# Attention and mixture-of-experts layer on one core: in the first chunk, the copies of the second eight heads' keys and queries wait for the first unit's rows of maxima

## The chip, the cores and the metric

The kernel runs on one core of one Trainium2 chip. A core has a matrix engine (TensorE, PE in the rows), a vector engine (VectorE, DVE), a scalar engine (ScalarE, ACT), a general engine (GpSimd, POOL), and a sync engine (SyncE, SP) that here only issues DMAs; each runs its own list of instructions in order, and they meet at semaphores. The metric is the time of one execution on the device in microseconds; lower is better.

## The reference, cut to what matters

One layer on 2048 tokens of 256 numbers: causal attention with 16 heads of 16 numbers, keys and values from a latent of 64, rotary embedding on 12 of 16 numbers of each head; then a layer norm, then a mixture of 16 experts (the best two for each token) with a shared expert, and a layer norm again.

```python
q = (x @ Wq).reshape(B, S, HEADS, HEAD_DIM).transpose(0, 2, 1, 3)
c_kv = x @ Wkv_down
k = (c_kv @ Wk_up).reshape(B, S, HEADS, HEAD_DIM).transpose(0, 2, 1, 3)
v = (c_kv @ Wv_up).reshape(B, S, HEADS, HEAD_DIM).transpose(0, 2, 1, 3)
...
qf = jnp.concatenate([q_nope, q_rope], axis=-1)
kf = jnp.concatenate([k_nope, k_rope], axis=-1)
scores = jnp.einsum('bhqd,bhkd->bhqk', qf, kf) * scale
scores = jnp.where(causal, -jnp.inf, scores)
weights = jax.nn.softmax(scores, axis=-1)
out = jnp.einsum('bhqk,bhkd->bhqd', weights, v)
...
x = _layernorm(x + _L0_attn_ref(x, ...), axis=-1)
x = _layernorm(x + _L0_ffn_ref(x, ...), axis=-1)
```

## The kernel before, in words

Attention goes by chunks of 512 queries (four) and in each by units of four heads (four a chunk, 16 in all). A unit takes steps, one for each block of 128 keys up to its chunk's end: 4 steps for each unit of chunk 0, 8 for those of chunk 1. In a step, `score_head` (line 1092) multiplies one block of keys with the 512 queries of each head, ScalarE takes the exponential (line 857), GpSimd clears what lies above the diagonal (`mask`, line 709), and every second step TensorE multiplies the probabilities of two steps with the values (`values`, line 1112). Scores go round three banks, so TensorE can be three heads ahead of ScalarE.

The softmax needs the maximum of each query's row before its first score. So each unit is computed twice: first `max_bank` (lines 1055 and 1060) makes its scores, VectorE takes maxima (lines 1312 and 1318) and folds them (1329), TensorE turns the column into rows (1035), VectorE writes them negated in two parts to `m_rows` (1372, 1373), and ScalarE's queue copies these two rows into `q_stack` below the queries (`store_maxima`, line 807, semaphore `m_stacked`, 16 for each of the two DMAs). The score matmul has 98 rows then, against 96 before. TensorE waits for `m_stacked` before a unit's first score.

Keys and queries are made in pieces. Piece n of a chunk: 0 keys and 1 queries of heads 0 to 7, 2 keys and 3 queries of heads 8 to 15. A piece is two jobs `("rope", c, 2n)` and `("rope", c, 2n + 1)`: TensorE projects (lines 970, 975, 983), ScalarE copies the bank to `rope_raw`, which has two buffers (line 819), the rotation makes three products and sums (`rotate`, lines 502, 503, 507; on VectorE in chunk 0, on GpSimd after it), and GpSimd splits the result in two parts in `kq_stage` (lines 642, 643, semaphore `kq_ready`). SP then runs `store_piece`: six DMAs that write the piece's parts, three copies of each half, to DRAM (line 552), and after a piece of queries the load of `k_stack` (line 559). `load_q` (line 530) loads the queries of a unit into `q_stack`. `load_tables` (line 541) loads the cosine and sine tables of the next chunk, which `rotate` needs.

The order of SP in chunk 0: pieces 0 and 1, `k_stack`, `load_q` of units 0 and 1, pieces 2 and 3, `k_stack`, `load_q` of units 2 and 3, `load_tables(1)`, then pieces 0 and 1 of chunk 1, `k_stack`, the next chunk's x, `load_q(4)`. A planner at the head of the program sets which bank of maxima and which job goes to which step, the same for all engines. By it the jobs before the first step are all of chunk 0's projections, the first latent of chunk 1, the maxima of unit 0, and ("rope", 1, 0); steps 0, 1 and 2 have ("rope", 1, 1), (1, 2) and (1, 3), step 2 also the maxima of unit 1. Unit 2's banks start in step 3, and unit 4's, the first of chunk 1, in step 9. After GpSimd's part of ("rope", 1, 0) come the load of the first tokens (line 653) and the mask of step 0, and from there masks and pieces by turns.

Of the kernel before, what the change touches and what calls it, by code (L numbers as in the profile page):

```python
# [59 lines left out]
def build_program(nc, t, out):  # L60
# [90 lines left out]
    for u in range(4, UNITS):  # L151
        c, g = divmod(u, UNITS_PER_CHUNK)
# [65 lines left out]
    with ExitStack() as ctx:  # L218
# [6 lines left out]
        def sem(name):  # L225
            return ctx.enter_context(nc.semaphore(name))
# [124 lines left out]
        m_stacked = sem("m_stacked")  # L351
# [158 lines left out]
        def _(sp):  # L510
# [32 lines left out]
            def store_piece(c, n):  # L543

                piece = 4 * c + n
                m, is_q = n // 2, n % 2

                sp.wait_ge(kq_ready, 2 * (piece + 1))
                for two in range(2):
                    rows = slice(two * (P // 2), (two + 1) * (P // 2))  # L550
                    for copy, part in enumerate((0, 1, 0) if is_q else (0, 0, 1)):
                        sp.dma_start(kq_dram[c, n, two, copy], kq_stage[rows, piece % 2, part].bitcast(F32))\
                          .then_inc(kq_stored[is_q], 16)
                if is_q:

                    sp.wait_ge(kq_stored[0], 16 * 6 * (piece // 2 + 1))
                    if piece > 1:
                        sp.wait_ge(k_stacked, 16 * (piece // 2))
                    sp.dma_start(k_stack[0:STACK, 4 * m:4 * m + 4, c * CH:(c + 1) * CH].bitcast(F32),
                                 kq_dram[c, n - 1].rearrange("two copy (d j) n -> (two copy d) j n", j=GH)).then_inc(k_stacked, 16)  # L560
                    sp.wait_ge(kq_stored[1], 16 * 6 * (piece // 2 + 1))
# [22 lines left out]
            for s in range(-1, END):  # L584
                for job in aux_at.get(s, ()):
                    if job[0] == "rope" and job[2] % 2:
                        store_piece(job[1], job[2] // 2)
                        if job[1] == 0 and job[2] % 4 == 3:
                            load_q(job[2] // 4 * 2)
                            load_q(job[2] // 4 * 2 + 1)  # L590
                        if job[2] == 3 and 0 < job[1] < NCH - 1:
                            load_chunk(job[1] + 1)
                        if job[2] == 7 and job[1] + 1 < NCH:
                            load_tables(job[1] + 1)
                for u in range(4, UNITS):
                    if q_load_at[u] == s:
                        load_q(u)

                if s == FREE_AT:
                    load_small()  # L600
                if s == FREE_AT + 20:
                    load_rows()
# [1214 lines left out]
```

## Time and profile before

| | us |
|---|---|
| median of 3 timed runs | 838.95 (837.67 to 840.08) |
| the profiled execution's own time | 838.23 |
| its span | 836.5 |
| TensorE busy | 720.1 (86%) |
| VectorE busy | 577.2 (69%) |
| ScalarE busy | 396.4 (47%) |
| GpSimd busy | 243.6 (29%) |

The span is the time from the first to the last instruction in the profile of one execution. Busy time says how much work an engine had, not that it was waited for: that is read from the chain of waits and from the timelines. A time in brackets behind an instruction is the idle time of its engine just ahead of it, with what ended it; "issue" there means nothing that the profile names.

### The profile page before, as it was taken

The numbers are of one execution on the slowest core, as the hardware profiler recorded it, in microseconds if no ns is written. First come the engines' busy times: TensorE is split into PE (matmuls) and PEld (weight loads), VectorE is DVE, ScalarE is ACT, GpSimd is POOL, SyncE is SP. The second block draws the span as 40 slices with busy tenths as digits, with TensorE's granted clock in tenths as the row PEclk, the third lists the DMA queues.
The fourth block names the chain that finished last, engine by engine and source line by source line (L and its number), as shares of the span: only waits on it lengthen the run. The fifth ranks groups of instructions, "written<-read, shape, count | busy, mean of one in ns | idle before, by whom it ended". The sixth has DMA issues, their size and how long they took to land.

```text
span 836.5 us, 13801 instructions
## 1 busy us (share of the span) xinstructions
PE 720.1 (86%) x4150; PEld 473.3 (57%) x4151; DVE 577.2 (69%) x1402; ACT 396.4 (47%) x848; POOL 243.6 (29%) x321
## 2 busy tenths in 40 slices
PE   4579899999999999999799999999839599999920
PEld 3467675664755666466355565544728466666610
DVE  6745779878789877776688888636616566665645
ACT  3125465555665756576466666668213122222203
POOL 6317172431261043107011010101650323333323
PEclk9659899999999999999899999999979799999965
DMA  4764315250051105001514800002950223333244
GB/s 130 170 158 109 97 40 139 80 130 20 2 128 51 52 1 138 16 1 39 132 43 123 263 2 1 20 2 69 318 207 2 83 77 94 97 95 95 82 170 157
DMA packets 43783, 75.96 MB, mean 91 GB/s; under 512 B 6004, under 2 KB 23668, under 8 KB 42860
## 3 DMA queue, kind: packets, MB, share of 16 engines
q1 hardware_dynamic: 36396, 57.75, 25.3%
q0 software_dynamic: 4896, 13.67, 4.8%
q10 hardware_dynamic: 2432, 3.80, 1.3%
q8 instruction: 31, 0.51, 0.3%
q14 instruction: 28, 0.23, 0.1%
HBM read 41.91 MB, written 32.93 MB: 89 GB/s over the span
## 4 chain that ended last, share of the span: by engine, by line
PE 64%; DVE 12%; issue 9%; DMA 6%; POOL 3%; ACT 3%; SPq 1%; ACTq 1%; another core or an unknown queue 1%; POOLq 0%; DVEq 0%
PE banks_ps L1055 15%; PE banks_ps L1112 14%; PE banks_ps L1092 12%; PE banks_ps L1152 7%; PE banks_ps L1188 5%; DVE mx L1318 4%; PE banks_ps L970 2%; PE banks_ps L1060 2%; PE banks_ps L1247 1%; ACT probs L857 1%; PE banks_ps L1165 1%; DMA q_stack<-kq_split 1%; DVE base L1739 1%; PE banks_ps L1176 1%; DMA token_y<-ys,dest 1%
## 5 line engine op out<-in xcount | busy, mean ns | idle before, releaser
L857 ACT ACTIVATE probs<-banks_ps 128x512 f32<-128x512 f32 (+3 forms) x640 | 302.4, 546 | 189.8 <-PE banks_ps L1092 173.8
L1318 DVE TENSOR_REDUCE mx<-banks_ps 128x1 f32<-128x512 f32 (+3 forms) x576 | 307.8, 593 | 72.4 <-PE banks_ps L1055 71.6
L1055 PE MATMUL banks_ps<-k_stack,q_stack 96*128 96x512 f32 (+3 forms) x832 | 251.2, 366 | 11.2 <-issue 5.6
L1092 PE MATMUL banks_ps<-q_stack,k_stack 98*128 98x512 f32 (+3 forms) x640 | 242.3, 397 | 17.3 <-ACT probs L857 11.4
L1055 PEld LDWEIGHTS banks_ps<-k_stack,q_stack 96*128 96x128 f32 x832 | 151.8, 202 | 89.8 <-issue 34.5
L1092 PEld LDWEIGHTS banks_ps<-q_stack,k_stack 98*128 98x128 f32 x640 | 122.7, 195 | 54.4 <-ACT probs L857 31.5
L1112 PE MATMUL banks_ps<-probs,v_ones 128*17 128x512 f32 (+3 forms) x1280 | 136.6, 543 | 1.1 <-POOL probs L709 0.9
L709 POOL TENSOR_SCALAR_AFFINE_SELECT probs<-probs 128x512 f32<-128x512 f32 x64 | 40.9, 639 | 325.0 <-ACT probs L857 324.8
L767 POOL DMA_INDIRECT token_y<-ys,dest x47 | 45.6, 970 | 96.8 <-DVE ys L1716 53.1
L1152 PE MATMUL banks_ps<-w_up_sb,xg_t 128*128 x188 | 67.9, 484 | 0.3 <-DVE hidden L1650 0.3
L1112 PEld LDWEIGHTS banks_ps<-probs,v_ones 128*17 128x17 f32 x1280 | 29.5, 98 | 67.5 <-issue 36.8
L1312 DVE TENSOR_REDUCE mx<-banks_ps 128x4 f32<-128x512 f32 x64 | 44.2, 690 | 31.0 <-PE banks_ps L1060 29.7
L1188 PE MATMUL banks_ps<-w_dn_sb,hidden_t 88*128 x188 | 49.3, 386 | 0.5 <-DVE ys L1716 0.5
L1703 DVE SCALAR_TENSOR_TENSOR part_w<-xg,expert_f 128x1 f32<-128x1 f32 x94 | 16.4, 216 | 44.3 <-DMA token_y<-ys,dest 39.5
L910 ACT ACTIVATE xg_t<-banks_ps 128x256 f32<-128x256 f32 x47 | 18.0, 383 | 56.9 <-PE banks_ps L1247 47.8
L1152 PEld LDWEIGHTS banks_ps<-w_up_sb,xg_t 128*128 128x128 f32 x188 | 32.4, 192 | 15.1 <-issue 1.7
L819 ACT ACTIVATE rope_raw<-banks_ps 128x512 f32<-128x512 f32 x32 | 19.2, 599 | 42.3 <-issue 20.3
L878 ACT ACTIVATE silu<-banks_ps 128x176 f32<-128x176 f32 x47 | 14.9, 317 | 45.7 <-PE banks_ps L1152 44.7
L1201 PE MATMUL banks_ps<-shared_dn,hidden_split 128*128 128x256 f32 (+1 forms) x144 | 22.5, 311 | 14.4 <-DVE hidden_split L1673 9.4
L1188 PEld LDWEIGHTS banks_ps<-w_dn_sb,hidden_t 88*128 88x128 f32 x188 | 32.3, 192 | 3.7 <-issue 1.0
L1165 PE MATMUL banks_ps<-x1t_first,shared_up 128*128 128x512 f32 (+1 forms) x108 | 27.5, 399 | 3.9 <-issue 3.9
L1201 PEld LDWEIGHTS banks_ps<-shared_dn,hidden_split 128*128 128x128 f32 (+1 forms) x144 | 20.6, 212 | 17.6 <-issue 8.6
(182 smaller groups left out, 727.8 us busy)
## 6 DMA issues: line engine op xcount, KB each, us to landing
kq_split<-kq_stage SPq DMA_DIRECT2D x96, 128.0 KB, 2.4
k_stack<-kq_split SPq DMA_DIRECT2D x8, 768.0 KB, 6.2
q_stack<-kq_split SPq DMA_DIRECT2D x32, 192.0 KB, 4.9
xg<-slot_x SPq DMA_DIRECT2D x47, 130.0 KB
slot_x<-blank SPq DMA_DIRECT2D x11, 520.0 KB, 8.6
w_up_sb<-w_up SPq DMA_DIRECT2D x4, 1408.0 KB
w_dn_sb<-w_dn SPq DMA_DIRECT2D x4, 704.0 KB
x_raw<-xT SPq DMA_DIRECT2D x4, 512.0 KB, 6.3
```

The source lines that it names most:

```text
L709: nc.gpsimd.affine_select(out=v, in_=v, compare_op=ALU.is_ge, fill=0.0, base=0, pattern=[[0, GH], [1, P]], channel_multiplier=-1).then_inc ...
L767: pool.indirect_dma_start(out=token_y, out_offset=bass.IndirectOffsetOnAxis(ap=dest[:, r:r + 1], axis=0), in_=ys[:, r, :], in_offset=None) ...
L857: nc.scalar.activation(probs[:, s % PROB_BUFS, h, off:CH], score_bank(n)[:, off:CH], ACT.Exp)\
L1055: ins = nc.tensor.matmul(dst[:, at:at + keys], q_stack[0:STACK, u % 4, h, tile * P:(tile + 1) * P], k_stack[0:STACK, pair, kb * CH + k0:kb ...
L1092: nc.tensor.matmul(score_bank(n)[:, off:CH], k_stack[:, 2 * g + h // 2, b * P:(b + 1) * P], q_stack[:, u % 4, h, off:CH], start=True, stop ...
L1112: last = nc.tensor.matmul(pv_ps[32 * h:32 * h + DH + 1, off:CH], v_ones[:, b, GH * g + h, :], probs[:, s % PROB_BUFS, h, off:CH], start=(b ...
L1152: last = nc.tensor.matmul(gate_ps[par][:, 0:2 * INTER], x_of(k), w_up[:, e, k, :], start=(k == 0), stop=(k == KT - 1))
L1165: last = nc.tensor.matmul(bank[n % 2][0:rows], shared_up[:, w, k, half, at:at + rows], x_of[:, a, k, tok], start=(m == 0), stop=(m == 3 * ...
L1188: last = nc.tensor.matmul(y_ps[par][:, 0:E], hidden_t[:, par, k, :], w_dn[:, e, k, :], start=(k == 0), stop=(k == 1))
L1201: last = nc.tensor.matmul(y_ps[i // 2][:, i % 2 * E:(i % 2 + 1) * E], hidden_split[0:rows, n % 2, a, i * P:(i + 1) * P], shared_dn[0:rows, ...
L1312: nc.vector.tensor_reduce(mx[:, u % 2, h * TPC:(h + 1) * TPC, c:c + 1], bank_of(bank).rearrange("p (i k) -> p i k", i=TPC), AX.X, ALU.max)\
L1318: last = nc.vector.tensor_reduce(mx[:, u % 2, h * TPC + tile, column:column + 1], bank_of(bank)[:, at:at + keys], AX.X, ALU.max)
```

## The change

One wait is added in SP's list, ahead of the first DMA of piece 2 of chunk 0 (the keys of heads 8 to 15). SP goes on only when both rows of maxima of unit 0 have landed in `q_stack`.

```diff
@@ -546,6 +546,9 @@
                 m, is_q = n // 2, n % 2
 
                 sp.wait_ge(kq_ready, 2 * (piece + 1))
+                if (c, n) == (0, 2):
+
+                    sp.wait_ge(m_stacked, 32)
                 for two in range(2):
                     rows = slice(two * (P // 2), (two + 1) * (P // 2))
                     for copy, part in enumerate((0, 1, 0) if is_q else (0, 0, 1)):
```

## Rows read from the trace of the kernel before

**Rows 1.** The page: TensorE's busy time, and its granted clock in 40 slices.

```profile
PE 720.1 (86%) x4150; PEld 473.3 (57%) x4151; DVE 577.2 (69%) x1402; ACT 396.4 (47%) x848; POOL 243.6 (29%) x321
...
PEclk9659899999999999999899999999979799999965
```

**Rows 2.** Chain of waits, 36 to 60 us: start us, us, what.

```profile
47.88 6.06 DMA q_stack<-m_rows
...
53.99 0.80 PE banks_ps L1092
```

**Rows 3.** Line 807, issues from 60 to 120 us: durations in ns, then landing.

```profile
L807 ACTq DMA_DIRECT2D q_stack<-m_rows x8: 510/566/691, 67.2 to 113.9; - x8
...
DMA to landing us min/median/max: 1.8/1.9/2.4
```

**Rows 4.** Timeline of SP's queue: start us, us, queue, line, operation, count.

```profile
37.45 8.93 SPq L552 DMA_DIRECT2D kq_split<-kq_stage  x12
46.47 0.60 SPq L559 DMA_DIRECT2D k_stack<-kq_split  x1
48.14 6.86 SPq L530 DMA_DIRECT2D q_stack<-kq_split  x4
55.05 0.63 SPq L541 DMA_DIRECT2D rope_sb<-rope  x1
...
68.93 12.30 SPq L552 DMA_DIRECT2D kq_split<-kq_stage  x12
...
83.53 8.02 SPq L530 DMA_DIRECT2D q_stack<-kq_split  x4
```

**Rows 5.** GpSimd's longest wait (total, times, longest), and landing of line 541's three issues.

```profile
POOL by_cos L502 <- DMA rope_sb<-rope: 25.4, 1, 25.4
...
DMA to landing us min/median/max: 4.3/6.5/7.0
```

**Rows 6.** Timeline of GpSimd, 56 to 80 us.

```profile
59.42 0.74 POOL L502 TENSOR_TENSOR by_cos<-rope_raw,rope_sb 128x256 f32<-128x256 f32 x1 [25.41 <-DMA rope_sb<-rope]
...
61.05 0.72 POOL L507 TENSOR_TENSOR roped<-by_cos,by_sin 128x256 f32<-128x256 f32 x1
...
63.88 1.39 POOL L709 TENSOR_SCALAR_AFFINE_SELECT probs<-probs 128x512 f32<-128x512 f32 x2
...
69.09 0.63 POOL L709 TENSOR_SCALAR_AFFINE_SELECT probs<-probs 128x512 f32<-128x512 f32 x1 [0.19 <-ACT probs L857]
...
76.83 0.73 POOL L643 TENSOR_TENSOR kq_stage<-roped,kq_stage 128x256 fp32r<-128x256 f32 x1
```

**Rows 7.** Chain at 87 us; landing of line 530's two issues from 83 us.

```profile
87.65 3.18 issue
...
DMA to landing us min/median/max: 6.4/6.6/6.7
```

**Rows 8.** Line 552, 36 to 47 us: min/median/max ns of an issue.

```profile
L552 SPq DMA_DIRECT2D kq_split<-kq_stage x12: 476/597/1990, 37.4 to 45.8; - x12
```

**Rows 9.** Timeline of ScalarE, 63 to 67 us.

```profile
66.19 0.60 ACT L819 ACTIVATE rope_raw<-banks_ps 128x512 f32<-128x512 f32 x1 [1.63 <-PE banks_ps L970]
```

**Rows 10.** Timeline of TensorE, 63 to 71 us.

```profile
63.83 2.32 PE L970 MATMUL banks_ps<-x_split,w_split 128*128 128x256 f32 x12
...
67.11 0.38 PE L1092 MATMUL banks_ps<-q_stack,k_stack 98*128 98x256 f32 x1 [0.50 <-ACT probs L857]
...
68.85 1.70 PE L1112 MATMUL banks_ps<-probs,v_ones 128*17 128x512 f32 x16
```

**Rows 11.** Stretches: length, busy (instructions) of each engine; clock, DMA share, GB/s.

```profile
65.00:65.50 0.50, 0.50 (x4) 0.50 (x4) 0.00 (x0) 0.00 (x0) 0.50 (x2) 0.53 0.56 229
...
89.00:89.50 0.50, 0.00 (x0) 0.00 (x0) 0.00 (x0) 0.00 (x0) 0.00 (x0) 0.86 0.77 164
...
96.00:96.50 0.50, 0.50 (x4) 0.41 (x3) 0.04 (x1) 0.50 (x3) 0.00 (x0) 0.81 0.08 17
```

## Prediction

> **What bounds the kernel now.** I read the page first: of a span of 836.5 us TensorE is busy 720.1 us, so the rule for most of the kernel is that a microsecond of TensorE is a microsecond of time [rows 1]. The same page shows that the first tenth is different: the granted clock is 0.5 in the third slice (42 to 63 us) and 0.6 in the one before, and TensorE's slices there are not full. The change sits in just that place, so the question is not what TensorE costs in total but which wait ends last between 37 and 91 us. Everything behind 91 us is the same instructions in the same order on every engine, with no outside clock: what these 54 us gain or lose stays in the time.
>
> The chain of waits shows the target of the change. The rows of maxima of unit 0 are issued on ScalarE's queue, the second at 47.88, and it lands after 6.06 us; TensorE's first score matmul starts behind it at 53.99 [rows 2]. Eight later issues of the same line landed in 1.8 to 2.4 us, median 1.9 [rows 3]. So about 4 us of the 6.06 are delay, and SP's queue shows what was in flight then: twelve copies of pieces 2 and 3 from 37.45, the k_stack load at 46.47, the q_stack loads from 48.14 [rows 4].
>
> The other half of the question is what stands behind those copies in SP's queue. SP runs its program in order: copies of piece 2, copies of piece 3, k_stack load, q_stack loads of units 2 and 3, then the rope tables of chunk 1, issued at 55.05 [rows 4]. The tables land 4.3 us later, at 59.35, and GpSimd has waited 25.4 us for nothing else when it starts (rope, 1, 0) at 59.42 [rows 5, 6]. GpSimd then works with one gap of 0.19 us to the end of its last piece at 77.56 [rows 6]. SP issues the rest of chunk 1's copies as these become ready, the last ending at 81.23, and the loads of chunk 1; the q_stack loads of unit 4 are issued from 83.53 and land after 6.4 to 6.7 us, so at about 90.6 [rows 4, 7]. TensorE, done at 87.65, stands still for 3.18 us and starts unit 4's banks at 90.83 [rows 7]. So there are two chains to 90.83: TensorE's own with 3.18 us to spare, and the chain of SP's queue, rope tables, GpSimd, copies, loads, which has nothing to spare. That second chain is the binding one, and it runs straight through the instruction that gets the new wait.
>
> **The change, part by part.** It removes nothing and adds one semaphore wait on SP, before the first copy of piece 2. What it does is move: all of SP from 37.45 on.
>
> 1. When does the wait end? The maxima do not depend on the held copies (their q_stack and k_stack come from pieces 0 and 1, on SP before the wait), so the second row is still issued at 47.88. With no copies in flight I take the median of the undisturbed issues, 1.9 us, and get 49.8; the ends are 1.8 and 6.06 us (49.7 and 53.9), the latter if the delay has another cause [rows 2, 3]. I take 1.9, since SP's last DMA ahead of the wait would be unit 1's q_stack load, issued by 37.4. SP's first copy moves from 37.45 to 49.8: later by 12.35 us.
>
> 2. Does SP run faster from there? The twelve copies took from 37.45 to 46.47, 9.02 us. Their median issue is 0.597 us, but one took 1.99 [rows 8]: it fell near the start of the twelve, while the q_stack loads of unit 1, issued just ahead of them, were moving. At 49.8 they have long landed. I take this stall as gone, minus 1.4 us; the ends are 0 and 1.4. The steps behind (stored copies landed, k_stack load, two pairs of q_stack loads) are a chain of the same transfers as before and I leave their length alone: 46.47 to 55.05. The rope tables are then later by 12.35 - 1.4 = 10.95 us: issued at 66.0, landed at 70.3. Their own landing stays at 4.3 us, the shortest of this line's three issues; were it the median, 6.5, 2.2 us would be added, but their neighbours in the queue are the same as before [rows 5].
>
> 3. What waits behind the tables? GpSimd's first product moves from 59.42 to 70.4. Queued behind it on GpSimd are the token load, the masks of steps 0 and 1 (63.88), and so on by turns of mask and rotation [rows 6]. They were a solid row of work, so they stay one; the 0.19 us gap for ScalarE goes, since ScalarE now has its exponentials of step 2 done at about 76 and that mask's turn comes at 80. Last piece ready: 77.56 + 10.95 - 0.19 = 88.3. Then the same copies and loads: unit 4 can start at 90.83 + 10.75 = 101.6.
>
> 4. What do the other engines do meanwhile? TensorE gets its first scores at about 49.85 instead of 53.99, a gain of 4.1 us, and runs the unit 1 banks 4 us early. But ScalarE's copy of (rope, 1, 2), at 66.19 before, waits until the rotation of (rope, 1, 0) has freed its buffer: that ended at 61.77, now at 72.7. ScalarE's exponentials stand behind it, and TensorE can be only three score banks ahead; so ScalarE resumes at 72.75, and TensorE's next score moves from 67.11 to about 73.7 [rows 9, 10]. The 4.1 us are eaten there. Then TensorE has the projection of (rope, 1, 3), 2.3 us at half clock, and the value matmuls of steps 0 and 1, which also need the masks (end 65.27, now 76.2): they start at 76.4 instead of 68.85 and take twice 1.70 us at half clock, to 79.8 instead of 70.55 [rows 6, 10]. TensorE is then 9.3 us late, and its work to 87.65 ends at 96.9; if the low clock lasts some 5 us more, at 99.5.
>
> [...]
>
> The sum: + 12.35 (wait) - 1.4 (queue stall) - 0.2 (gap) = + 10.75 us. The profiled execution took 838.23 us (span 836.5 and 1.7 around it), so it would take 849.0. The three timed runs have a median of 838.95, 0.72 above it; on that scale I forecast 849.7 us. Its own bounds are +9.5 (queue faster by another 1.2) to +13.7 (landing at 2.4, no stall regained, GpSimd's row longer by 1.0): 848.4 to 852.6.
>
> [...]
>
> **The rivals.**
>
> A. The maxima land no sooner: the 6.06 us are not contention with these copies. Then SP starts at 53.95, later by 16.5, and the sum is 16.5 - 1.4 - 0.2 = + 14.9: 853.9. Against it: eight issues of 1.8 to 2.4 [rows 3]. 5%.
>
> B. TensorE reaches unit 4's banks so near to the loads that it doesn't stand. Before, the clock fell within 2 us of standing and TensorE then had 5.4 us at half clock [rows 7, 11]. Kept at full clock it would save up to 2.6 us, and the shift is about 10.75 - 2.6 = + 8.2: 847.1. By my numbers it stands 2.1 to 4.7 us, so the clock falls; 12%.
>
> C. The held copies meet other traffic, or slow-clocked TensorE passes the loads and becomes the bound; each costs 2 to 3 us: + 13.3, 852.3. The slack in step 4 speaks against it. 13%.
>
> D. The change gains: the loads of chunk 1 have slack, and the 4.1 us of earlier scores [rows 2] remain. It decides from the point where SP's chain has those 10.95 us to spare; with all of them spare the time is 838.95 - 4.1 = 834.9. GpSimd's wait of 25.4 us for the tables and TensorE's stand at 87.65 say it has none [rows 5, 7]. 4%.
>
> E. The wait is passed without delay, or SP's delay just cancels the gain: no change, 839. The rows were issued at 47.28 at the earliest and SP stood ready at 37.45 [rows 2, 4], so this would need an error in my reading of the order. 3%.
>
> **The numbers.** Forecast 849.7 with 63%, then A to E. A 0.3% of 838.95 is 2.5 us, about what a measurement of this kernel can tell from no change. Faster by more: 4%; within: 3%; slower: 93%. The range from 846.4 to 853.6 takes in the forecast's own bounds, B and C, and leaves out A, D, E and some of the tails.
>
> **What would show it.** Right: a hole in SP's issues from 37.4 to about 49.8; the second row landing in about 1.9 us; the first score matmul near 49.9; rope tables issued near 66; GpSimd's wait for them grown from 25.4 to about 36 us; TensorE standing from about 63 to 73 us and again before unit 4's first bank at about 101.6; every later stage shifted by the same amount. Wrong: the k_stack and q_stack loads of unit 2 taking clearly less than from 46.47 to 55.05, GpSimd starting before 68, or unit 4's banks starting on TensorE's own time without a wait.

## Result and profile after

The changed kernel takes 849.14 us (median of 4 runs, 848.48 to 850.10); the kernel before, on the same chip, 838.53 (4 runs, 837.67 to 840.08). The ratio is 1.0125, 95% interval 1.0106 to 1.0145: slower by 10.6 us. The profiled execution has a span of 846.8 us against 836.5.

The whole execution after has its attention 0.89 us later from the start (first bank of maxima at 37.75 against 36.86 us), which is not the change's: SP had not reached the wait. Distances below are therefore taken from that matmul where it matters.

SP's queue of the changed kernel (start us, us, queue, line, operation, count), which answers to [rows 4]:

```profile
31.32 6.97 SPq L530 DMA_DIRECT2D q_stack<-kq_split  x4
50.70 7.52 SPq L555 DMA_DIRECT2D kq_split<-kq_stage  x12
58.32 0.60 SPq L562 DMA_DIRECT2D k_stack<-kq_split  x1
60.00 6.75 SPq L530 DMA_DIRECT2D q_stack<-kq_split  x4
66.79 0.63 SPq L541 DMA_DIRECT2D rope_sb<-rope  x1
80.83 12.11 SPq L555 DMA_DIRECT2D kq_split<-kq_stage  x12
93.04 0.59 SPq L562 DMA_DIRECT2D k_stack<-kq_split  x1
```

The hole between the first line's end (38.29) and 50.70 is the wait. Behind it, down to the tables, every step has its old length within 0.2 us, but for the twelve copies, which take 7.62 us to the next issue against 9.02.

The chain of waits of the changed kernel, 36 to 106 us, cut to its links (start us, us, what), answers to [rows 2]:

```profile
48.77 1.86 DMA q_stack<-m_rows
...
57.62 2.36 DMA kq_split<-kq_stage
...
60.37 5.59 DMA q_stack<-kq_split
...
66.79 4.67 DMA rope_sb<-rope
...
71.53 0.72 POOL by_cos L502
...
88.50 0.74 POOL kq_stage L646
...
93.04 6.08 DMA k_stack<-kq_split
```

The chain no longer goes through TensorE's scores: maxima landed, copies, queries' loads, tables, GpSimd, copies, loads. It reads as the order of SP's list.

GpSimd, ScalarE and TensorE after, for [rows 6, 9, 10 and 7]:

```profile
71.53 0.72 POOL L502 TENSOR_TENSOR by_cos<-rope_raw,rope_sb 128x256 f32<-128x256 f32 x1 [36.93 <-DMA rope_sb<-rope]
...
73.94 0.60 ACT L822 ACTIVATE rope_raw<-banks_ps 128x512 f32<-128x512 f32 x1 [13.84 <-POOL roped L507]
...
50.68 0.80 PE L1095 MATMUL banks_ps<-q_stack,k_stack 98*128 98x512 f32 x1 [0.32 <-DMA q_stack<-m_rows]
...
74.87 0.58 PE L1095 MATMUL banks_ps<-q_stack,k_stack 98*128 98x256 f32 x1 [13.38 <-ACT probs L860]
...
102.46 0.75 PE L1058 MATMUL banks_ps<-k_stack,q_stack 96*128 96x512 f32 x1 [4.22 <-issue]
```

The first score matmul has nothing to wait for any more (0.32 us). But TensorE then stands 13.38 us behind ScalarE, ScalarE behind GpSimd, and GpSimd behind the tables, 11.5 us longer than before. The last line is the point that counts: unit 4's first bank at 102.46 against 90.83. Less the 0.89 us of the head that is 10.74 us.

### The profile page after: what moved, and what is told of

The parts are those of the page before. It is cut to its first block, busy times and chain, and to the rows that moved or that the text cites. A ratio compares the mean times of both kernels' runs of the same rounds, so it can differ in the third digit from the quotient of the medians.

```text
span 846.8 us, 13802 instructions
## 1 busy us (share of the span) xinstructions
PE 724.4 (86%) x4150; PEld 477.1 (56%) x4151; DVE 577.0 (68%) x1402; ACT 396.5 (47%) x848; POOL 244.3 (29%) x321
## 4 chain that ended last, share of the span: by engine, by line
PE 62%; DVE 11%; issue 8%; DMA 7%; POOL 5%; SPq 2%; ACT 2%; ACTq 1%; POOLq 0%; DVEq 0%
PE banks_ps L1058 13%; PE banks_ps L1115 13%; PE banks_ps L1095 11%; PE banks_ps L1155 7%; PE banks_ps L1191 5%; DVE mx L1321 3%; PE banks_ps L1168 3%; DMA q_stack<-kq_split 2%; SPq L555 2%; PE banks_ps L1204 2%; PE banks_ps L1250 2%; PE banks_ps L1063 1%; PE banks_ps L973 1%; ACT probs L860 1%; PE banks_ps L1179 1%
## 5 line engine op out<-in xcount | busy, mean ns | idle before, releaser
L1155 PEld LDWEIGHTS banks_ps<-w_up_sb,xg_t 128*128 128x128 f32 x188 | 32.4, 192 | 14.7 <-issue 2.0
L1204 PE MATMUL banks_ps<-shared_dn,hidden_split 128*128 128x256 f32 (+1 forms) x144 | 24.3, 320 | 12.6 <-issue 7.6
L502 POOL TENSOR_TENSOR by_cos<-rope_raw,rope_sb 128x256 f32<-128x256 f32 x24 | 17.5, 729 | 44.0 <-DMA rope_sb<-rope 36.9
```

The source lines that it names most:

```text
L1155: last = nc.tensor.matmul(gate_ps[par][:, 0:2 * INTER], x_of(k), w_up[:, e, k, :], start=(k == 0), stop=(k == KT - 1))
L1204: last = nc.tensor.matmul(y_ps[i // 2][:, i % 2 * E:(i % 2 + 1) * E], hidden_split[0:rows, n % 2, a, i * P:(i + 1) * P], shared_dn[0:rows, ...
```

## Experiments

Each kernel was timed in turns with the kernel before on one chip, and the ratio is to that. Chips differ: the kernel before took 823.8 us on the chip of e1 to e4, 837.8 on that of c0 and e5 to e7, 839.6 on that of e8 and e9. "Unit 0 to unit 4" is the distance between their first banks of maxima in the profile, 53.97 us in the kernel before. It comes from one profile each, and two profiles of one kernel differ in it by 0.5 us (the change and c0), 0.7 (e1 and e8) and 2.8 (e3 and e9).

| kernel | unit 0 to unit 4, us | to before | ratio (95%) |
|---|---|---|---|
| the change | 64.71 | +10.74 | 1.0125 (1.0106 to 1.0145) |
| c0, the change again | 64.24 | +10.27 | 1.0136 (1.0111 to 1.0160) |
| e1, tables ahead, wait kept | 49.79 | -4.18 | 0.9984 (0.9957 to 1.0011) |
| e8, e1 again | 50.51 | -3.46 | 0.9963 (0.9942 to 0.9983) |
| e2, tables ahead, no wait | 53.73 | -0.24 | 0.9994 (0.9970 to 1.0017) |
| e3, tables ahead, only the k_stack load waits | 47.54 | -6.43 | 0.9939 (0.9914 to 0.9963) |
| e9, e3 again | 50.34 | -3.63 | 0.9941 (0.9916 to 0.9966) |
| e4, released later | 69.41 | +15.44 | 1.0161 (1.0129 to 1.0194) |
| e5, only the tables held | 64.73 | +10.76 | 1.0101 (1.0076 to 1.0127) |
| e6, only the k_stack load waits, tables behind | 57.47 | +3.50 | 1.0048 (1.0031 to 1.0065) |
| e7, tables ahead, released later | 60.17 | +6.20 | 1.0045 (1.0023 to 1.0066) |

**e1: the tables taken out from behind the wait.** The edit against the kernel before:

```diff
                 sp.wait_ge(kq_ready, 2 * (piece + 1))
+                if (c, n) == (0, 2):
+                    load_tables(1)
+                if (c, n) == (0, 2):
+                    sp.wait_ge(m_stacked, 32)
...
-                        if job[2] == 7 and job[1] + 1 < NCH:
+                        if job[2] == 7 and 0 < job[1] and job[1] + 1 < NCH:
                             load_tables(job[1] + 1)
```

> The wait of the change stays; only the load of chunk 1's rope tables is moved in SP's list from behind the q_stack loads of units 2 and 3 to just ahead of the wait. Theory (the tables are what the wait makes late): tables issued near 38 and landed by 44; second row of maxima lands in about 1.9 us, first scores near 50 as with the change; GpSimd no longer waits for tables at 60, its row of work follows the masks and so runs 4 us earlier than in the kernel before; unit 4's first bank near 86.7 against 90.83; time 838.5 - 4.1 = 834.4, range 833.4 to 836. Rival 1 (the held copies and the loads of units 2 and 3 cost time themselves): time stays above 845. Rival 2 (unit 2's banks then wait for their loads, which land near 66, and take the gain back): 837 to 839.

SP's queue and TensorE of e1:

```profile
37.46 0.65 SPq L541 DMA_DIRECT2D rope_sb<-rope  x1
48.64 7.57 SPq L556 DMA_DIRECT2D kq_split<-kq_stage  x12
56.31 0.60 SPq L563 DMA_DIRECT2D k_stack<-kq_split  x1
...
48.67 0.79 PE L1096 MATMUL banks_ps<-q_stack,k_stack 98*128 98x512 f32 x1 [0.32 <-DMA q_stack<-m_rows]
...
86.59 0.76 PE L1059 MATMUL banks_ps<-k_stack,q_stack 96*128 96x512 f32 x1 [3.80 <-issue]
```

The same copies are held nearly as long as in the change (10.5 us from the end of the issue before, 12.4 there), and unit 4's bank comes at 86.59, where 86.7 was expected. Moving one DMA turns + 10.7 us into - 4.2. The loss of the change is not in the held copies. They are felt in one place: GpSimd stands 3.73 us until its stage buffer is stored, but it has to wait for exponentials a little later anyway (2.36 us). The time missed its range: 0.9984 with an interval around 1, where 0.994 to 0.997 was expected, lies in that of rival 2. That rival's mechanism is not there, since TensorE begins unit 2's banks at 65.99 without a stand. The gain was clear in the profile and not in that timing, so it was timed again (e8).

**e2: the tables moved, without the wait.** As e1 without the `sp.wait_ge(m_stacked, 32)` and its `if`.

> The kernel before without the wait, but with the tables' load ahead of the copies of piece 2. Theory: the second row of maxima still lands late (near 54, 6 us), the mask of step 1 still holds GpSimd's second rotation at about 65, so nothing is gained: 838.5, range 837.5 to 839.5. Rival (the tables alone were worth time in the kernel before, since GpSimd waits 25.4 us for them): 834 to 836. If theory and the first kernel of this call both hold, the wait is worth its 4 us only together with the move of the tables.

As expected: no difference (- 0.24 us at unit 4, 0.9994). The rows of maxima land late as before, and GpSimd, which now has its tables, waits for ScalarE's exponentials instead:

```profile
53.49 0.80 PE L1094 MATMUL banks_ps<-q_stack,k_stack 98*128 98x512 f32 x1 [4.62 <-DMA q_stack<-m_rows]
...
64.14 0.64 POOL L711 TENSOR_SCALAR_AFFINE_SELECT probs<-probs 128x512 f32<-128x512 f32 x1 [4.07 <-ACT probs L859]
```

In the kernel before, the tables and the rows of maxima were late by about the same, so that taking away the tables' lateness alone gives nothing. The prediction had called the tables' chain the one that binds; the rows, exponentials and masks bind beside it.

**e3: which traffic delays the rows of maxima?** Tables ahead; copies at once; the wait only ahead of the second k_stack load.

```diff
                         sp.wait_ge(k_stacked, 16 * (piece // 2))
+                    if piece == 3:
+                        sp.wait_ge(m_stacked, 32)
```

> Tables first; the copies of pieces 2 and 3 go at once, and the wait for the maxima stands only ahead of the k_stack load of heads 8 to 15 (768 KB). It tells which traffic delays the rows of maxima. If the k_stack load does: the second row lands in about 2 us, scores near 50, time 834.5 (range 833.5 to 836). If the copies do (the last are issued at 46 and land by 48.5): the row lands in 4 us or more, time 836.5 to 838.5.

The landing in the chain of e3 is as short as with all twelve copies held:

```profile
49.30 1.86 DMA q_stack<-m_rows
```

SP's queue of e3:

```profile
39.62 8.69 SPq L554 DMA_DIRECT2D kq_split<-kq_stage  x12
51.24 0.60 SPq L563 DMA_DIRECT2D k_stack<-kq_split  x1
51.95 7.88 SPq L530 DMA_DIRECT2D q_stack<-kq_split  x4
```

The last copy's issue ends at 48.31, 1 us before the second row's, and the copies do not delay it. What does is what came behind them, the k_stack load of 768 KB or the first queries' loads; no run holds one of these without the other. SP's stand shrinks to the 2.9 us before 51.24, and the ratio is 0.9939, the lowest of the table.

**e4: a later release, tables behind.** The change with `sp.wait_ge(pe_scores, 4)` in place of the wait for the maxima.

> The change with a later release: SP waits for TensorE's fourth score matmul in place of the rows of maxima, some 5.2 us later (55.9 against 50.7). Theory (from the release on one chain sets the time): every us of hold is a us of time, so 849.1 + 5.2 = 854.3, range 853 to 855.5. Rival (some of the hold is hidden): under 852.

```profile
55.32 7.54 SPq L554 DMA_DIRECT2D kq_split<-kq_stage  x12
...
71.39 0.63 SPq L541 DMA_DIRECT2D rope_sb<-rope  x1
...
106.49 0.63 PE L1057 MATMUL banks_ps<-k_stack,q_stack 96*128 96x512 f32 x1 [3.95 <-issue]
```

The copies start at 55.32. From the turning of unit 0's maxima (TensorE, the transpose before `m_rows`) to the first copy it is 8.86 us against 3.58 in the change, 5.28 longer; unit 4 comes 4.70 later than in the change (69.41 - 64.71). Nearly one for one. In time it is 1.0161, 13.3 us on this chip's 823.8 (10.6 to 16.0 by the interval), where 15.8 were expected, 14.5 at least. The rival (some of the hold is hidden) stood for less than 13.5, so the time leaves it open; only the profile speaks for one to one.

**c0: the change again, e5: only the tables held.** e5 is the kernel before with one wait ahead of `load_tables(1)`:

```diff
+                        if job[2] == 7 and job[1] == 0:
+                            sp.wait_ge(pe_scores, 9)
                         if job[2] == 7 and job[1] + 1 < NCH:
                             load_tables(job[1] + 1)
```

> The changed kernel once more, beside the three others of this call: its ratio to the kernel before should again be near 1.0125, and unit 4's first bank of maxima near 102.5 us; its landing of the rows of maxima near 1.9 us.

> The kernel before; copies and loads of pieces 2 and 3 go at once as there, only the load of the rope tables is held in its place, until TensorE's ninth score matmul (near 66 us, where the change had issued it). Theory (the late tables alone are the loss): tables 11.2 us later than before, unit 4's first bank near 102, time 838.5 + 11.2 = 849.7, ratio 1.013. Rival (the late copies and loads of units 2 and 3 are the loss): ratio under 1.003.

c0 repeats the change (1.0136; unit 4 at 101.34). In e5 copies and loads run at once, as before, and the tables alone are late:

```profile
47.51 6.75 SPq L530 DMA_DIRECT2D q_stack<-kq_split  x4
65.46 0.63 SPq L541 DMA_DIRECT2D rope_sb<-rope  x1
...
101.92 0.77 PE L1057 MATMUL banks_ps<-k_stack,q_stack 96*128 96x512 f32 x1 [5.54 <-issue]
```

The late tables by themselves put unit 4 where the change puts it (+ 10.76 against + 10.74). The parts agree less closely: counted from unit 0's first bank the tables are 10.1 us late here and 10.85 in the change, and unit 4's bank comes 8.5 us after the first issue of its loads, against 7.3. The rival, under 1.003, is out. The ratio, 1.0101, lies under the 1.013 expected, but its interval overlaps that of c0 on the same chip; whether the 2.5 us between their medians are real is not settled.

**e6: e3's wait without moving the tables.**

> The kernel before with the wait for the maxima ahead of the k_stack load of heads 8 to 15 alone; the copies go at once and the tables stay behind the loads. The rows of maxima should land in 1.9 us and scores begin near 50, but SP stands from 46.5 to 49.9, so the tables are issued 3.4 us later, near 58.5. Theory (the chain through the tables sets the time whatever TensorE gains): unit 4's first bank 3.2 us later, 841.7, ratio 1.004. Rival (the 4 us of earlier scores count): ratio 0.995.

```profile
50.02 0.60 SPq L561 DMA_DIRECT2D k_stack<-kq_split  x1
50.74 7.64 SPq L530 DMA_DIRECT2D q_stack<-kq_split  x4
58.43 0.63 SPq L541 DMA_DIRECT2D rope_sb<-rope  x1
...
63.34 0.72 POOL L502 TENSOR_TENSOR by_cos<-rope_raw,rope_sb 128x256 f32<-128x256 f32 x1 [29.68 <-DMA rope_sb<-rope]
```

The tables are 3.4 us later, unit 4 3.5 us, and the time 1.0048 (4.0 us). Scores began at 49.99, 4 us early, and it brought nothing. With the change and e4 this gives three doses of one cause: counted from unit 0's first bank, tables issued later by 3.2, 10.9 and 16.1 us, and unit 4 later by 3.5, 10.7 and 15.4.

**e7: tables ahead, and a hold of 17 us.**

> Tables first, and the copies of pieces 2 and 3 held until TensorE's fourth score matmul (near 55.5), 6.9 us longer than with the maxima. Theory: without the tables behind it the hold costs only by the stage buffers (GpSimd's split of the next piece waits until the copies of piece 2 have landed, near 61): GpSimd is then where it is in the kernel before, unit 4's first bank near 90.4, ratio 0.9995. Rival (each us of hold is a us of time, as with the tables behind): ratio above 1.012.

Both expectations missed: 1.0045, and + 6.20 at unit 4, between them. The chain, SP's queue and TensorE show a wait that I had not priced:

```profile
62.17 7.71 DMA k_stack<-kq_split
69.89 1.30 issue
71.19 1.09 PE banks_ps L1059 x4
...
66.28 5.61 SPq L530 DMA_DIRECT2D q_stack<-kq_split  x4
...
71.19 1.09 PE L1059 MATMUL banks_ps<-k_stack,q_stack 96*128 96x128 f32 x4 [6.10 <-issue]
```

TensorE stands 6.10 us ahead of unit 2's first bank. The k_stack load of heads 8 to 15 has landed at 69.88, but the bank begins 1.3 us later: last come unit 2's queries, whose second load, issued at 66.7, lands after 4.4 us, at about 71.1. GpSimd's wait for its stage buffer, 9.01 us, came as the theory said. So there is a second limit behind the tables: a hold until the maxima (e1, e8) brings no stand ahead of unit 2, and one 17 us long makes the held loads themselves awaited; where between them it begins was not tried. In the change they were not awaited (unit 2's banks came behind the longer wait for the tables).

**e8 and e9: e1 and e3 again.**

> Tables first and the wait where the change has it, timed again beside the other version, since the first timing left a gain of 4.2 us at unit 4's first bank as 0.2% with an interval around zero. Theory (the 4.2 us stay, less what phases of low TensorE clock in the last unit give back, about 2 us in that profile): ratio 0.9945 to 0.9985. Rival (they are lost behind the attention): 0.9985 or more.

> Tables first, only the k_stack load held, timed again. Theory: 0.991 to 0.996 as in the first timing, unit 4's first bank 5 to 6 us earlier than before by the distance from the turning of unit 0's maxima. Rival (the first timing was luck, the true gain is that of the other version): 0.996 to 0.998.

e8 gives 0.9963 (0.9942 to 0.9983) and e9 0.9941 (0.9916 to 0.9966). e3's version is faster than the kernel before in both timings, by 5 us (e9: 834.41 against 839.60 us, 12 and 23 runs), and so is the best version here. That it beats e1's is not shown; the intervals overlap. One expectation of e9 missed: from the turning of unit 0's maxima to unit 4 it takes 3.6 us less than the kernel before (40.96 against 44.60), not 5 to 6; in e3 it was 6.4 less.

## Why the prediction was right

The forecast was 849.7 us and + 10.75; measured were 849.14 and + 10.6. By its steps:

1. **When the wait ends.** Right, and the reason too: the second row landed 1.86 us after its issue (1.9 taken). The clock times are 0.9 us later than written (50.70 against 49.8) because the whole execution was.
2. **The copies run faster.** Right: 7.62 against 9.02 us, the 1.4 us taken. The tables were issued 66.79 - 55.05 = 11.74 later, less 0.89: 10.85, for 10.95. They landed in 4.67 us, for 4.3.
3. **GpSimd.** Right: from its first product to the end of its last piece 17.70 us (71.53 to 89.23), before 18.14. The gap of 0.19 went as said; the other 0.25 us (0.15 of it in the two first masks, 1.24 for 1.39) was not foreseen and made up for most of the tables' slower landing. That the shift at unit 4 is 10.74 for 10.75 is luck to this extent: - 0.1 (issue), + 0.37 (landing), - 0.25 (GpSimd) and - 0.04 (copies and loads) cancel.
4. **TensorE and ScalarE.** Right in mechanism: the 4 us of early scores ended in a stand of 13.38 us behind the copy of (rope, 1, 2). TensorE resumed at 74.87 (73.7 forecast, 74.6 with the head), and reached the loads at 98.24, inside the 96.9 to 99.5 given (97.8 to 100.4 with the head); it stood 4.22 us.
5. **The clock.** Half right, without effect on the sum. Step 4 takes TensorE at half clock behind the stand, through the value matmuls and up to 5 us more. The granted clock fell in the stand (0.50 from 66 us to the restart at 74.87), but it rose sooner than I assumed, by 79 us:

```profile
64.00:66.00 2.00, 0.00 (x0) 0.00 (x0) 0.00 (x0) 0.00 (x0) 0.00 (x0) 0.73 0.42 78
...
78.00:79.00 1.00, 1.00 (x9) 0.20 (x12) 0.00 (x0) 0.00 (x0) 0.92 (x2) 0.71 0.28 111
```

These are stretches of the changed kernel with columns as in [rows 11]. The value matmuls took 1.99 us, not the 3.4 forecast for them at half clock. That TensorE stood again before unit 4 rules out rival B in the profiled execution. No run shows B's saving of 2.6 us: behind that stand of 4.22 us the granted clock was 0.50 from 103 to 109 us, as it was from 90 to 96 us in the kernel before.

Rival A (maxima land no sooner) fell with the 1.86 us, D (SP's chain has slack) with e5 and e6, where later tables move the time; of C's two mishaps neither shows, the held copies landing in 2.2 to 2.4 us (2.3 to 4.2 before) and TensorE standing at unit 4 in each run with the tables behind. E fell with the result. One reading of the start of the prediction was too strong: that GpSimd waits 25.4 us for nothing but the tables and that their chain alone binds. With the tables early, e2 gains 0.24 us, because GpSimd then waits 4.07 us for ScalarE behind the late rows. The forecast didn't suffer, since the change makes the tables later still. On the cause of the late rows the first guess was too wide: "copies in flight" were named with the loads, and e3 shows that the copies are innocent. How the loads delay the rows is not shown: the runs have only the landing of the second row, 6.06 us in the kernel before and 1.86 in the change and in e3, where the loads were held.

What the argument got by luck is the rest of the kernel. The shift at unit 4 is 11.6 us between the two profiles and 10.3 at the end, but not steadily so: it was 12.2 when unit 6's maxima were turned, 9.6 at unit 15's, and 11.6 at the last scores. The last section shows two of the steps, 1.6 us less and 2.0 us more. Between the last scores and the end the shift shrinks by another 1.3 us, behind the attention, and that is not explained. So the premise that what these 54 us lose stays in the time holds only to 1 or 2 us.

## What to carry to other kernels

Before a wait is put into a queue that runs in order, list everything behind it and find who waits for the last item, not the first: here the delayed copies were not missed for a long time, and a table load seventeen issues further down set the time. If that item doesn't depend on what is waited for, put it ahead; the same wait then gave 3.5 to 4.2 us at unit 4, and 0.2 to 0.4% of the time, instead of taking 11 us. And hold the large transfer that is really in the way, not the small ones ahead of it: that costs SP 3 us of standing, not 12.

## What the runs showed of the hardware that was not expected

**Phases of low clock wander.** TensorE's granted clock falls to half (0.50 at 342 to 344 us in the kernel before) for some us at places that differ between executions, with the same work. In the last unit, at equal points of the work, before and after (stretches of 4 us, columns as in [rows 11]):

```profile
540.00:544.00 4.00, 3.33 (x30) 2.03 (x29) 1.94 (x3) 2.83 (x8) 1.09 (x2) 1.00 0.31 98
544.00:548.00 4.00, 3.93 (x32) 2.66 (x28) 2.80 (x6) 3.36 (x8) 0.00 (x0) 1.00 0.00 0
```

```profile
549.60:553.60 4.00, 2.93 (x15) 2.16 (x15) 1.38 (x2) 3.32 (x10) 1.27 (x2) 0.93 0.33 100
553.60:557.60 4.00, 4.00 (x28) 2.41 (x26) 1.55 (x3) 1.69 (x5) 0.00 (x0) 0.64 0.00 0
```

After the change the clock fell there, behind a stretch in which TensorE was busy 2.93 of 4 us, and 2.0 us were lost; in the kernel before it did not, after 3.33 of 4. At 342 to 346 us it was the other way round: the kernel before had

```profile
342.00:344.00 2.00, 2.00 (x13) 0.49 (x16) 0.10 (x1) 1.07 (x3) 0.64 (x1) 0.50 0.00 0
```

and the changed one no low clock at the same work (1.00 from 353.6 to 357.6 us), which gave back 1.6 us. There TensorE had been busy 2.60 of the 4 us ahead in both (338 to 342 and 349.6 to 353.6 us). e3 and e9, one kernel, differ by 2.8 us at unit 4, and in e3 the clock had risen by 58 us (0.86 at 57 to 58, 1.00 behind it), in e9 only at about 63 (0.50 until then, 0.82 at 63 to 64). So a difference of 1 to 3 us between two profiles of this kernel is no evidence; the medians of several runs are.

**A stand with no releaser.** The kernel before took 823.8 us on the chip of e1 and 838.5 on that of its profile. In that profile VectorE stands from 609.5 to 623.1 us for nothing that the profile names; in e1's, at the same work, its only wait of that kind is 0.2 us:

```profile
623.10 0.69 DVE L1666 TENSOR_TENSOR wide_hidden<-wide_silu,banks_ps 128x512 f32<-128x512 f32 x1 [13.58 <-issue]
```

Other engines work meanwhile: of 609.5 to 623.1 us TensorE is busy 4.93 and GpSimd 8.96. The later scatter of tokens on GpSimd shows the same gap in every profile: it waits 13.5 to 14.7 us for VectorE in the four on the chip of e1, and 27.5 to 29.5 us in the eight on the other chips. That has the size of the difference between the chips. Its cause stays open.
